# Fused patch embedding, linear attention and top-2 expert layer on one core: choices, an early table and a root moved at the seam between the image steps and the expert tiles

## The reference

```python
h = _L0_tok_ref(x, gamma, beta, W, b)                          # 64 x 169 x 128
h = h + _L0_attn_ref(_layernorm(h), Wqkv, Wout, bout, proj)    # 8 heads, exp features, denominators D
h = h + _L0_ffn_ref(_layernorm(h), Wg, W, V, W2)
# in the expert block
gate_logits = jnp.einsum('bsd,de->bse', x, Wg)                 # 8 experts
topv, topi = jax.lax.top_k(gate_logits, 2)
w = jax.nn.softmax(topv, axis=-1)
h = silu(x @ W[e]) * (x @ V[e]);  y += gw[..., e] * (h @ W2[e])
```

## Time and profile before

| | |
|---|---|
| median of three runs | 1143.21 us |
| the profiled execution | 1143.8 us, span 1142.0 us |
| TensorE matmul busy | 1089.6 us, 95% of the span |
| VectorE busy | 882.1 us, 77% |
| GpSimd busy | 614.4 us, 54% |
| ScalarE busy | 561.5 us, 49% |
| TensorE by 40 slices of 28.6 us, tenths | 3999999999999999999999979999999999999996 |
| granted TensorE clock, the same slices | 9 in all but the last, which has 8 |

### The profile page before, as it was taken

The page is one execution under the profiler, slowest core; times in us unless marked ns, Lnnn a source line. Parts: engine busy times, 40 slices in busy tenths (PEclk is TensorE's granted clock), DMA queues, the critical chain, the costliest instruction groups (busy, mean ns, idle before and its releaser), DMA issues.

```text
span 1142.0 us, 30063 instructions
## 1 busy us (share of the span) xinstructions
PE 1089.6 (95%) x8628; PEld 924.8 (81%) x8629; DVE 882.1 (77%) x3333; ACT 561.5 (49%) x1307; POOL 614.4 (54%) x656
## 2 busy tenths in 40 slices
PE   3999999999999999999999979999999999999996
PEld 3677777777777777777776669999999999999996
DVE  5568887887888878878868677777777777777774
ACT  3545535536345354363333425555555555555552
POOL 0103545445445444454444466676767676677675
PEclk9999999999999999999999999999999999999998
DMA  8270131311301213011110424343443443444443
GB/s 166 51 203 22 38 74 32 80 30 33 81 31 35 77 30 82 27 36 30 33 30 31 114 72 75 47 58 53 55 51 53 55 56 53 53 53 54 54 56 31
DMA packets 76012, 65.53 MB, mean 57 GB/s; under 512 B 12338, under 2 KB 66802, under 8 KB 75926
## 3 DMA queue, kind: packets, MB, share of 16 engines
q0 software_dynamic: 32704, 24.99, 15.7%
q1 hardware_dynamic: 43078, 39.16, 13.9%
q10 hardware_dynamic: 144, 0.32, 0.1%
HBM read 32.72 MB, written 31.71 MB: 56 GB/s over the span
## 4 chain that ended last, share of the span: by engine, by line
PE 79%; DVE 11%; issue 3%; DMA 3%; ACT 1%; SPq 1%; POOL 1%; DVEq 0%; POOLq 0%; another core or an unknown queue 0%; ACTq 0%
PE bank L1472 20%; PE bank L1495 13%; PE bank L690 7%; PE bank L739 5%; PE bank L752 5%; PE bank L620 4%; PE bank L726 4%; PE bank L728 3%; PE bank L727 3%; PE bank L745 3%; PE bank L477 2%; PE bank L708 2%; DVE rparts L930 2%; PE bank L613 2%; DMA out_rows<-yo,dest 2%
## 5 line engine op out<-in xcount | busy, mean ns | idle before, releaser
L1666 POOL DMA_INDIRECT out_rows<-yo,dest x184 | 312.5, 1699 | 138.0 <-issue 103.7
L1472 PE MATMUL bank<-xT_e,wv 128*128 128x256 f32 x2208 | 288.5, 286 | 2.4 <-DVE xT_e L1583 2.2
L1472 PEld LDWEIGHTS bank<-xT_e,wv 128*128 128x128 f32 x2208 | 270.8, 189 | 2.9 <-DVE xT_e L1583 2.4
L1349 POOL DMA_INDIRECT sorted_rows<-xrow_all,sloti x192 | 192.0, 1000 | 77.5 <-issue 58.0
L1553 ACT ACTIVATE sil<-bank 128x256 f32<-128x256 f32 x368 | 141.0, 385 | 168.3 <-PE bank L1472 149.5
L1495 PE MATMUL bank<-w,hid 128*128 x1472 | 181.4, 277 | 4.4 <-DVE hid L1590 4.0
L1495 PEld LDWEIGHTS bank<-w,hid 128*128 128x128 f32 x1472 | 173.0, 193 | 5.8 <-issue 5.7
L1572 DVE TENSOR_TENSOR wv<-wv_all,wv 128x1024 fp32r<-128x1024 f32 x92 | 113.3, 1232 | 65.4 <-PE bank L1472 51.2
L1590 DVE TENSOR_TENSOR hid<-sil,bank 128x256 f32<-128x256 f32 x368 | 143.8, 417 | 25.2 <-ACT sil L1553 21.3
L1256 ACT ACTIVATE attn<-bank 128x256 f32<-128x256 f32 x128 | 49.5, 387 | 161.5 <-issue 123.4
L1534 ACT CAST wv<-wv_all 128x1024 fp32r x92 | 96.2, 1046 | 30.7 <-issue 28.2
(11 more groups left out here) (216 smaller groups left out, 1816.0 us busy)
## 6 DMA issues: line engine op xcount, KB each, us to landing
xr<-sorted_rows SPq DMA_DIRECT2D x92, 130.0 KB
raw<-in_x SPq DMA_DIRECT2D x64, 84.5 KB
raw<-in_x SPq DMA_DIRECT2D x60, 78.0 KB
out_rows<-attn SPq DMA_DIRECT2D x64, 58.5 KB
sorted_rows<-xrow_all,sloti POOLq DMA_INDIRECT x192
out_rows<-yo,dest POOLq DMA_INDIRECT x184
wv_all<-in_L_ffn_W SPq DMA_DIRECT2D x8, 256.0 KB, 5.1
wv_all<-in_L_ffn_V SPq DMA_DIRECT2D x8, 256.0 KB, 5.3
```

Source lines behind the costliest of these rows:

```text
L1349: po.indirect_dma_start(sorted_rows, bass.IndirectOffsetOnAxis(sloti[:, p, j, ch:ch + 1], 0), xrow[:, p, j, ch], None).then_inc(s(f"scatte ...
L1472: q = pe.matmul(bank[fc][:, TT * m:TT * m + TT], wv[:, w, w_, m, cols], xT[:, p, x_], start=(w_ + x_ == 0), stop=(w_ == 1))
L1666: po.indirect_dma_start(out, bass.IndirectOffsetOnAxis(dest[:, p, a:a + 1], 0), yo[:, p, a], None, compute_op=ALU.add).then_inc(s(f"added{ ...
```

## The change

Six edits, all at the seam but for one that reaches back to step 30.

1. `early_table` is cut in two. `early_counts`, its first nine operations, runs in step 30, and the remaining eleven, still called `early_table`, in step 31; both stand between the normalised rows and the row statistics.
2. In step 32 `choose` stands behind two of the four quarters, no longer ahead of them.
3. In step 33 `choose` stands behind all four quarters, no longer ahead of `dsum`; `normal_rows` stands behind it. TensorE's `rank()` of step 33 moves from ahead of the broadcasts to between the output products of the two images.
4. Low weights: those of tile 1 are made in step 32 (before: step 33), those of tile 2 in step 33 (before: tile step 1).
5. In step 33 GpSimd's root stands ahead of all six scatters of the pair, no longer behind three.
6. Unread products: 6 instead of 9 in step 33, and 1 instead of 3 ahead of the rank in step 34.

The diff, cut to its core (the waits that each new function starts with are as they were):

```diff
@@ TensorE, step
                 if n == NPAIR + 1:
-                    idle_products(9)
+                    idle_products(6)
                     expert_tensor(pe, "turn")
                 if n == NPAIR + 2:
                     expert_tensor(pe, "first")
-                    idle_products(3, 4)
-                if d and not a and not b:
+                    idle_products(1, 4)
+                if n == NPAIR + 2:
                     rank()
...
-                    if a and d and i == 1:
+                    if d and i == (1 if a else 0) and (a or n == NPAIR + 1):
                         rank()
@@ VectorE, step
-                if n == NPAIR + 1:
-                    choose(md)
...
-                    normal_rows()
-                if n == NPAIR:
-                    choose(md)
+                    if n != NPAIR + 1:
+                        normal_rows()
...
                 if c:
                     normalise(1)
+                if n == NPAIR:
+                    choose(md)
...
                 if c:
                     normalise(3)
-                if d and a:
+                if d and a or n == NPAIR + 1:
                     choose(md)
+                if n == NPAIR + 1:
+                    normal_rows()
...
                     place(md, pd, 96 * half(-3))
+                if n == NPAIR:
+                    expert_vector(ve, "weights", range(1, 2))
                 if n == NPAIR + 1:
-                    expert_vector(ve, "weights", range(1, 2))
+                    expert_vector(ve, "weights", range(2, 3))
...
                 if d and a:
                     normal_rows()
+                if n == NEARLY_PAIRS + 2:
+                    early_counts()
+                if n == NEARLY_PAIRS + 3:
+                    early_table()
...
-                if n == NEARLY_PAIRS + 2:
-                    early_table()
@@ GpSimd, step
                     wait_alone(po, setup_met, (s("sloti_ready"), md + 1), (s("w1_ready"), md + 1))
-                    scatter(range(1))
-                    if c:
-                        scatter(range(1, 2), which=(0,))
+                    if not c:
+                        scatter(range(1))
                 if c:
...
                     root(rstd[:, 1], mv[:, 1, :, 1], vare[:, 1], 1e-5, K("mhalf")[:, 0:NCH], s("ln2_vare"), s("ln2_rstd"), mc)
                 if d and not late:
                     wait_alone(po, setup_met, (s("sloti_ready"), md + 1))
+                    if c:
+                        scatter(range(1))
+                    scatter(range(1, 2), which=(0,))
                     if not c:
-                        scatter(range(1, 2), which=(0,))
@@ VectorE, tile step
-            if more and not (isinstance(t, int) and t < 1):
+            if more and not (isinstance(t, int) and t < 2):
                 low_w(t + 1, (w + 1) % 4)
```

More of the change, by code:

```diff
@@ L1030, in best, with early_chain, early_counts @@
                 ve.wait_ge(s("gap_whole"), m + 1)
-            def early_table():
+            early_link = [0]
+            def early_chain(q):
+                early_link[0] += 1
+                q.then_inc(s("early_step"), 1)
+                ve.wait_ge(s("early_step"), early_link[0])
+            def early_counts():
+                chain = early_chain
                 ve.wait_ge(s("colsum_ready"), 4 * NG)
                 ve.wait_ge(s("counts_ready"), NEARLY_PAIRS)
-                link = [0]
-                def chain(q):
-                    link[0] += 1
-                    q.then_inc(s("early_step"), 1)
-                    ve.wait_ge(s("early_step"), link[0])
-                n_, t_ = slice(0, R1), K("steps")
+                n_ = slice(0, R1)
                 chain(ve.tensor_tensor(early_has, counts[n_].unsqueeze(2).to_broadcast([R1, E, FIRST_TILES]),
@@ L1054, in early_table @@
                 chain(ve.tensor_tensor(early_more, early_of[:, 1:E + 1], early_of[:, 0:E], ALU.subtract))
+            def early_table():
+                chain = early_chain
                 chain(ve.tensor_tensor(early_past, K("tile")[0:1].unsqueeze(2).to_broadcast([1, FIRST_TILES, E]),
```

## The result

The changed kernel took 1139.28 us in the median of 22 runs (1135.9 to 1142.43), the kernel before 1142.24 us in 22 runs beside it (1139.18 to 1146.2). The ratio is 0.9972, with a 95% interval from 0.9962 to 0.9982: about 3 us faster. The forecast was 1135.7 us and a gain of 7.5 us; the measured median lies 0.3 us above the top of the range. The forecast was counted from three runs' 1143.21 us; from the 1142.24 us of 22 runs the same gain would give 1134.7 us, so by gains the miss is 4.5 us: 3.0 measured, 7.5 forecast.

A forecast was written before the change was run, and what follows sets the result against it. TensorE was taken as busy, with gaps at the seam behind other engines. Early steps 6.1 plus tiles 1.4 gave 7.5 us off 1143.8, so 1136.3; less 0.6 for the median, 1135.7 us, range 1134.0 to 1139.0.

The forecast's parts named there:

- Steps 31 and 32: TensorE's waits go: 2.41 us by the early table in two, 1.48 us by the choice behind two quarters.
- Step 33: Choice behind the quarters, rank between the two images: VectorE is the bound, and this part costs 0.1 us.
- rival C: TensorE's clock falls behind idle time in step 33 or at tile 3, 1.6 us per fall; chance 0.15.
- if the clock fell in step 33: Named sign that the prediction would be wrong: a fall of TensorE's granted clock in that step.
- The early stretch: Gains summed through step 34, forecast at 6.1 us; under 5 us was a named sign of being wrong.
- Step 34: With GpSimd's root ahead of six scatters, the choice's 2.31 us wait for the root goes.
- The gaps operation: Named sign: in step 34 it stands right behind the choice's first half.
- Tiles 1 to 5: Tile 3's down product starts 1.4 us sooner, set by tile 0's additions landing; 1.0 to 1.9 by landing time.
- rival D: GpSimd's 2.01 us wait for landed scatters grows by 2.7 because six go out in a row; chance 0.07.
- The stall behind the empty tiles: TensorE stalls until 740 behind the additions of empty tiles 5 to 8; it moves along whole, and all after it.

The follow-up runs named there:

- f3: The kernel before with only the early table in two pieces and step 32's choice behind two quarters: 1136.53 us, ratio 0.9963.
- e1: The changed kernel with four more unread products ahead of the gate products in step 33: 1139.1 us, ratio 0.997.
- f1: The changed kernel with step 33's root again behind three scatters, not ahead of all six: 1135.57 us, ratio 0.9945.
- g1: The kernel before with only step 33's root moved ahead of all six scatters: 1140.91 us, ratio 0.999.
- g3: The changed kernel with four buffers instead of two for scaled rows and indices, and the root back behind three scatters: 1131.99 us, ratio 0.9912.
- f4: The changed kernel with four buffers instead of two for scaled rows and indices, and four more unread products in step 33: 1132.99 us, ratio 0.9923.
- e3: The changed kernel with four more unread products in step 33 and seven around tile 5's transposes: 1136.15 us, ratio 0.9937.
- g2: The changed kernel with four buffers for scaled rows, four more unread products in step 33 and the root back behind three scatters: 1132.82 us, ratio 0.9919.

## Why the prediction was wrong in size

**Steps 31 and 32: right.** Forecast 2.41 and 1.48 us, measured 2.54 and 1.60; f3, which has only these, 4.3 by the rank of step 34.

**Step 33: about right.** The gate products were to come 0.1 us later than before beside the earlier gains, and came 0.56 later (gain 3.58 at L708, 4.14 ahead of it). VectorE was the bound, as worked out. The fall behind the 2.08 us wait then added 0.77 us (1.73 - 0.96 for L708). That was rival C's first place, and by the prediction's own signs it was wrong from there: "if the clock fell in step 33". The early stretch gave 5.02 us, just above the 5 that it named as the other sign.

**Step 34: the term was 2.31 and measured 1.44** (from L708 to the rank, 7.63 us before and 6.19 after). The gaps operation waits for nothing, as forecast, so the mechanism was right; the fall took the missing 0.8: in e1, where it doesn't come, the same stretch takes 5.42 us, a gain of 2.21. Against f1 the edit is worth 0.9 here, since f1's wait was down to 1.78 and f1 had no such fall in L708.

**Tiles 1 to 5: the step that failed.** It forecast a further gain of 1.4 us at tile 3, which measured 0.26 (5.28 - 5.02), and nothing lost behind it, where 2.4 us went. It had the first addition start at 683.5, that is 76.7 us behind step 30's rank. It started at 79.09. Of the 2.4 us, 1.1 are the root's: forecast at 56.9 (63.01 before, less the 6.1 gained), it ran at 57.99, held up for the most part by the fall in step 33 (ScalarE's copy behind L708 came late, and VectorE waited 1.20 us for it; in e1, without the fall, the root runs at 57.27). The other 1.2 are GpSimd's wait for landed scatters, 3.20 us where I had kept 2.01. In size that is rival D at under half its price, but D's reason, six scatters in a row, isn't what the runs show: g1 has six in a row and waits 1.72 us, f1 and g3 have them apart and wait 2.63 and 2.96. What lengthens this wait stays open. The addition landed after 3.44 us, forecast 3.8. So tile 3 came 2.2 us later than forecast, and still by the mechanism that the text named.

Then came what the sum didn't hold at all: behind 1.16 and 2.33 us of idle time the clock fell, and tile 4 came 2.4 us later still. I had given a fall 0.15 as rival C, at 1.6 us each; they cost 0.8 and 2.4. For step 33 I had worked out 1.6 us of idle time ahead of the gate products and for tile 3 1.5, both less than the 2.19 that stood ahead of the old fall; they became 2.08 and 3.49. Nor was the old wait a measure: falls stood behind waits of 0.60 us too (f4, g3). The mistake was to treat the additions' lateness (rival D) and the clock (rival C) as separate accidents: a late addition lengthens the very gap behind which the clock falls, so the two come together, and their sum had to be the main case or the one next to it. With the 0.77 us of step 33, the 1.2 of the landing wait and the 2.4 at tile 3, the forecast's 7.5 becomes 3.1; the profiles gave 2.8 behind the empty tiles and the medians 3.0. By the Trainium skill (TensorE: Matmul & The Clock Gate, what's actually happening) half rate is the rest state that recent activity lifts; the trace agrees with that, 0.50 to 0.59 behind both gaps.

**What the sum credited wrongly.** It counted edit 5 as plus 2.31 us, and took its price on GpSimd's queue, 3.8 - 0.4 us, as one that the earlier edits had for the most part paid for. How much GpSimd had to spare stands in the kernel before, on VectorE's timeline and GpSimd's:

```profile
694.38 0.25 DVE L1596 CAST dest<-meta_ 128x2 uint32<-128x2 f32 x1
```

```profile
688.14 1.58 POOL L1666 DMA_INDIRECT out_rows<-yo,dest  x1 [0.31 <-issue]
```

The second addition, landed after some 3.44 us at 691.6, left 2.8 us until VectorE scaled tile 2 at 694.38 without a wait. Edit 5 by itself makes the additions 2.6 us later (g1, from step 31's rank), and gives a wait of 1.91 us. The other edits alone bring VectorE to that place 6.9 us sooner (f1: the wait starts at 80.72, the scaling of before stood at 87.57) and the first addition 2.9 us sooner, and give a wait of 1.78 us. Both together gave 4.97. Without the edit the kernel is 3 us faster (f1), and the remaining five edits give 6.3 us, 0.0055 of 1141.6.

The stall behind the empty tiles moved along whole, as forecast: 41.69 us before, 41.75 after.

## What to carry to other kernels

When several edits each take a wait off the same engine, recompute the slack of the other engines after all of them: an operation moved ahead of a queue's ready work costs that queue its whole wait (here 4.1 us of an idle GpSimd), and what was slack before is the bound after. Where a sum leaves idle time of TensorE, and the trace has one slow stretch behind such a gap, count a fall as the likely case and add what the next products take at half rate: of the 14 profiles 12 had a fall somewhere from step 31 to tile 4, and the two without one (e3, g2) have the gap of step 33 filled and none left open at tile 3 (as has f4, which had one). Unread products in the gap gave that back at tile 3 without removing the wait; in step 33 no median showed them. If a wait is for a buffer, a second pair of buffers can be worth more than any order of the work: here 6 us on top of the change.

## What the runs showed that I had not expected

- A fall of the clock cost 2.4 us behind 1.16 and 2.33 us of idle time with only two transposes between them, and 0.8 behind a single 2.08. f1 had a wait of 2.12 us at that same place in step 33 and its L708 still took 0.96; its fall came behind L708 and was no smaller (clock 0.92 from 655 to 665 us, 0.91 from 665 to 675). In step 31 the same wait of 2.22 us was followed by no fall in the kernel before and by one in g1. So the same gap doesn't bring the same fall in every execution, and a profile of one execution can't price it.
- Indirect additions of 64 KB landed after 3.44 us (changed kernel) and 4.10 us (f1: 686.37 to 690.47), in line with the 3.31 to 4.24 of the earlier trace rows. The Trainium skill (DMA: Bandwidth & Descriptors, anatomy of one DMA) would have 2.15 us as an estimate; no run here came near it.
- The time up to step 30 varied by 6.3 us between profiles of kernels that are equal up to there (603.18 to 609.52). That is twice what the change gained, so single executions had to be compared from a common marker, and g1 shows that even behind the marker one profile can be off by 1.5 us.
